# Rows normalised on ScalarE, a gate bias in 16-bit halves, a re-ordered last stage and a summary taken in pairs of tiles, in a two-layer attention and FFN kernel

## What is computed

```python
# layer 0 attention: softmax over 1601 context keys + 256 causal keys, 16 heads of 128, 4 key/value heads
q, k = rope(rms_norm(x @ wq)), rope(rms_norm(x @ wk)); k_ctx = rms_norm(ctx @ wk_ctx)
out = softmax(q @ [k_ctx, k].T * scale + mask) @ [ctx @ wv_ctx, x @ wv] @ wo
# layer 0 FFN: rows rotated by a Hadamard matrix, quantised to 8 bits; weights ternary
h = silu(bitlinear(x, w_gate)) * bitlinear(x, w_up); out = bitlinear(h, w_down)
# layer 1 attention: linear attention over the context, phi(x) = x + 1 if x > 0 else exp(x)
k, v = split(ctx @ Wkv.T); kv_summary = einsum('bhsd,bhse->bhde', phi(k), v); k_sum = phi(k).sum(-2)
gate = sigmoid(x @ Wg.T + bg)
attn = (phi(x @ Wq.T) @ kv_summary) / (phi(x @ Wq.T) . k_sum + eps); out = (attn * gate) @ Wo.T
# layer 1 FFN: 8 experts, top 2 per row by a softmax router
```

## Time and profile before

| | |
|---|---|
| median of 3 runs | 1352.47 us (1347.48 to 1353.33) |
| the profiled execution | 1355.68 us, of which its span is 1353.6 us |
| PE busy | 1215.0 us, 90% |
| DVE busy | 1021.0 us, 75% |
| ACT busy | 823.1 us, 61% |
| POOL busy | 761.6 us, 56% |

### The profile page before, as it was taken

How to read it: one execution, slowest core, us unless ns; L and a number is a source line. 1 busy time by engine, 2 the same in 40 slices (tenths; PEclk the granted TensorE clock), 3 DMA queues, 4 the chain that set the end, 5 groups by cost and what they waited for, 6 DMA issues and landing times.

```text
span 1353.6 us, 30595 instructions
## 1 busy us (share of the span) xinstructions
PE 1215.0 (90%) x11443; PEld 914.0 (68%) x11443; DVE 1021.0 (75%) x2067; ACT 823.1 (61%) x1916; POOL 761.6 (56%) x964
## 2 busy tenths in 40 slices
PE   3888789999999999999999999999999556778898
PEld 2555467877777777877778777777777444455557
DVE  5777678788878887878788788877888485973654
ACT  3555577767767676676767677677676452453331
POOL 2000386857758586675867658586686375822210
PEclk9999899999999999999999999999999787886899
DMA  7531068687977879788786876878778891000000
GB/s 250 169 102 38 1 118 148 125 148 136 178 144 126 141 128 145 133 177 138 136 148 125 140 137 126 147 122 151 137 130 148 177 214 26 1 1 1 0 1 31
DMA packets 499933, 156.99 MB, mean 116 GB/s; under 512 B 484800, under 2 KB 493776, under 8 KB 499792
## 3 DMA queue, kind: packets, MB, share of 16 engines
q1 hardware_dynamic: 497664, 147.77, 58.9%
q0 software_dynamic: 2128, 7.35, 2.1%
HBM read 29.12 MB, written 4.33 MB: 25 GB/s over the span
## 4 chain that ended last, share of the span: by engine, by line
PE 67%; DVE 15%; DMA 6%; POOL 5%; ACT 4%; issue 3%; SPq 0%; POOLq 0%; ACTq 0%; DVEq 0%
PE PS L1164 13%; PE PS L1166 13%; PE PS L1165 13%; PE PS L1320 7%; PE PS L1316 7%; PE PS L1317 7%; DVE mx L1648 4%; DMA pT_h<-ph 3%; DMA pT_l<-pl 2%; DVE pl L1668 2%; POOL xn L891 2%; PE PS L1269 1%; PE PS L665 1%; ACT ctx_h L1393 1%; POOL rstd L888 1%
## 5 line engine op out<-in xcount | busy, mean ns | idle before, releaser
L1648 DVE TENSOR_REDUCE mx<-PS 128x1 f32<-128x512 f32 (+2 forms) x512 | 297.0, 622 | 137.6 <-PE PS L1166 136.4
L1316 PE MATMUL PS<-v_h,pT_h 128*128 128x129 f16 (+1 forms) x1856 | 229.4, 224 | 23.2 <-DMA pT_h<-ph 13.7
L1317 PE MATMUL PS<-v_l,pT_h 128*128 128x128 f16 (+1 forms) x1856 | 229.4, 222 | 0.0
L1864 POOL CAST ph<-pr_end 128x705 f16<-128x705 f32 (+1 forms) x128 | 109.1, 853 | 184.5 <-ACT pr_end L1459 171.7
L1316 PEld LDWEIGHTS PS<-v_h,pT_h 128*128 128x128 f16 (+1 forms) x1856 | 184.5, 99 | 27.5 <-DMA pT_h<-ph 15.2
L1164 PE MATMUL PS<-kT_h,qT_h 128*128 128x512 f16 (+2 forms) x512 | 182.0, 356 | 7.3 <-ACT pr L1459 7.3
L1317 PEld LDWEIGHTS PS<-v_l,pT_h 128*128 128x128 f16 (+1 forms) x1856 | 184.7, 100 | 2.5
L1459 ACT ACTIVATE pr<-PS,nb 128x1024 f32<-128x1024 f32 x128 | 144.0, 1125 | 64.9 <-DVE nb L1656 64.9
L1165 PE MATMUL PS<-kT_l,qT_h 128*128 128x512 f16 (+2 forms) x512 | 181.2, 354 | 0.0
L1166 PE MATMUL PS<-kT_h,qT_l 128*128 128x512 f16 (+2 forms) x512 | 181.1, 354 | 0.0
L1668 DVE TENSOR_TENSOR pl<-pr,ph 128x1024 f16<-128x1024 f32 x128 | 172.5, 1348 | 0.0
(11 more groups left out here) (287 smaller groups left out, 2969.4 us busy)
## 6 DMA issues: line engine op xcount, KB each, us to landing
stage<-in_ctxT SPq DMA_DIRECT2D x8, 800.5 KB, 5.3
lanes<-in_w_lanes SPq DMA_DIRECT2D x16, 192.0 KB, 4.2
stage<-in_wq SPq DMA_DIRECT2D x4, 512.0 KB, 3.7
stage<-in_wo SPq DMA_DIRECT2D x4, 512.0 KB, 3.9
pT_h<-ph SPq DMA_TRANSPOSE x128, 4.3
pT_l<-pl SPq DMA_TRANSPOSE x128, 4.2
ctx_kept<-ctx_h SPq DMA_DIRECT2D x2, 800.5 KB, 6.7
ctx_kept<-ctx_l SPq DMA_DIRECT2D x2, 800.5 KB, 8.3
```

What stands on the lines that cost most here:

```text
L1316: mm(PS[:, OB, 0:DH + 1], pT_h[0:rows, slot, t, :], v_h[0:rows, par, v, :], start=t == 0, stop=False)
L1317: mm(PS[:, OB, 0:DH], pT_h[0:rows, slot, t, :], v_l[0:rows, par, v, :], start=False, stop=False)
L1648: dve.reduce_max(mx[:, c:c + 1], PS[:, c, 0:cols(u % LT, c)], AX_X).then_inc(mx_part, 1)
L1864: pool.tensor_copy(ph[:, slot, HALF:LAST + w], pr_end[:, 0:BANK + w]).then_inc(pool_hi, 1)
```

## The change

- The summary runs in 28 steps of up to two tiles (seven to a sequence, the 65-row tile last). ACT reads k from PSUM twice, for exp(k/64 + ln 64) and for relu(k), and casts v to float16; DVE takes min(exp, 64) + relu in one operation, and v's low half; POOL casts the sum to float16 and subtracts for its low half; PE adds three float16 products instead of one float32 product. All is scaled by 64, and the summary by 1/64 at the end. Some buffers are three deep, and the summary of a step is issued after the projection two steps later.
- The loop starts as soon as items 0, 1 and 2 are split. SP issues Wkv's load ahead of x's. The normalising and transposing of x stand inside the first steps, the products for the rope tables inside POOL's steps 7 to 10, the other splits after steps 0, 2, 3 and 5 of each sequence.
- In the last stage POOL makes per row the factor and a shift, -mean * factor (`row_scales`, two more small operations), and ACT normalises: Identity with scale and bias. `nm` moves from TAIL_POOL to TAIL_ACT.
- The gate's bias is two float16 rows, added by two float16 matmuls.
- TAIL_PE, TAIL_ACT and TAIL_DVE have new orders, the splitting of the last group's ternary weights comes after that unit's `out_norm`, and `dn1:03` (so half 0's last `az`) is the last step of all.
- The first preparing jobs take other PSUM banks.

```diff
-    qt:12 qt:13 dn0:10 dn0:11 lq:00 dn0:12 dn0:13 lq:01 tr1:10 tr1:11 la:00 la:01 la:02 la:03 lg:10
...
+    dn0:11 tr1:01 dn0:12 dn0:13 lq:00 lq:01 tr1:10 lg:00 tr1:11 lg:01 lg:10 lg:11 la:00 la:01 la:02
+    la:03 lq:10 lq:11 tr3:00 tr3:01 lo:00 lo:01 la:10 la:11 la:12 la:13 tr2:00 tr3:10 tr2:01 tr3:11
...
+    nm0:00 nm0:01 hi0:00 hi0:01 cq:00 cq:01 nm0:10 si0:00 hi0:10 nm0:11 si0:01 hi0:11 si0:02 si0:03
+    cq:10 cq:11 hx0:00 si0:10 hx0:01 si0:11 hx0:02 si0:12 hx0:03 si0:13 hx0:10 hx0:11 ro:00 ro:01 hx0:12
+    hx0:13 ro:02 ro:03 ct:00 ct:01 ct:02 ro:10 ro:11 ct:03 nm1:00 hi1:00 ro:12 ro:13 ct:10 ct:11 nm1:01
+    ct:12 ct:13 hi1:01 nm1:10 lc:00 lc:01 hi1:10 nm1:11 sg:00 hi1:11 sg:01 ex:00 ex:01 sg:10 sg:11 lc:10
...
-    nm0:00 nm0:01 nm0:10 nm0:11 b1:00 b1:01 bp:01 b1:02 b1:03 bp:03 b1:10 b1:11 bp:11 b1:12 b1:13 bp:13
...
+    rs0:00 rs0:01 rs0:10 rs0:11 b1:00 b1:01 bp:01 b1:02 b1:03 bp:03 b1:10 b1:11 bp:11 b1:12 b1:13 bp:13
...
+L1_STEPS = (CT + 1) // 2
+L1_ALL = B * L1_STEPS
+L1_LOADS = {0: 0, 2: 1, 3: 2, 5: 3}
+LN_AT = 2
...
-                after(B - 1)
+        def l1_tiles(n):
+
+            t = n % L1_STEPS
+            return [((2 * t + j) * P, P) for j in range(2)] if t < L1_STEPS - 1 else [((CT - 1) * P, CREM)]
+
+        def l1_shape(n):
+            tiles = l1_tiles(n)
+            return len(tiles), tiles[0][1]
+
...
                     o = token_tile(hf, 0, j)
-                    mm(o, ones[0:1, :], bgs[:, :], start=True, stop=False)
+                    mm(o, ones16[:, :], bg_h[:, :], start=True, stop=False)
+                    mm(o, ones16[:, :], bg_l[:, :], start=False, stop=False)
                     for c in range(DC):
...
+            def norm(n, hf, p):
+                act.wait_ge(tl[f"rs{n}"], nth(f"rs{n}", hf, p))
+                for j in (2 * p, 2 * p + 1):
+                    t = hf * 4 + j
+                    last = act.activation(xn4[hf][:, j, :], x_tile(hf, j), ACT.Identity, scale=rstd[:, t:t + 1],
+                                          bias=shift[:, t:t + 1])
+                last.then_inc(tl[f"nm{n}"], 1)
...
-                for j in (2 * p, 2 * p + 1):
-                    t = hf * 4 + j
-                    last = pool.tensor_scalar(xn4[hf][:, j, :], x_tile(hf, j), mv[:, t, 0:1], rstd[:, t:t + 1],
-                                              ALU.subtract, ALU.mult)
-                last.then_inc(tl[f"nm{n}"], 1)
+                step(pool.tensor_tensor(shift[:, at], mv[:, at, 0], rstd[:, at], ALU.mult))
+                pool.tensor_tensor(shift[:, at], shift[:, at], minus[:, at], ALU.mult).then_inc(tl[f"rs{n}"], 1)
...
-                         x.rearrange("(t p) d -> p t d", p=P)).then_inc(in_x, 16)
             for i, (parts, n, scale, hi, lo) in enumerate(loads):
+                if i == 1:
+                    sp.dma_start(xs[:, :].rearrange("p (t d) -> p t d", t=TILES),
+                                 x.rearrange("(t p) d -> p t d", p=P)).then_inc(in_x, 16)
...
+            def l1_proj(n):
+                b = n // L1_STEPS
+                if n % L1_STEPS == 0:
+                    pe.wait_ge(set_lo, FIRST if b == 0 else FIRST + 4 * (b - 1) + 2)
+                wait(pe, l1_vl, n - 1)
+                for j, (col, rows) in enumerate(l1_tiles(n)):
+                    for c in range(DC):
+                        last = three(PS[0:rows, n % 2 * 2 + j, :],
...
-                              vf_s[0:nrows, par, c, :], start=first, stop=final)
+            def l1_summary(n):
+                b, t, slot = n // L1_STEPS, n % L1_STEPS, n % 3
+                m, rows = l1_shape(n)
+                if t == 0:
+                    wait(pe, l1_R, b - 1)
+                    if b == 1:
+                        pe.wait_ge(ln_lo, 4)
+                pe.wait_ge(l1_vl, n + 1)
+                pe.wait_ge(l1_lo, n + 1)
+                for j in range(m):
+                    for c in range(DC):
+                        o = PS[:, (TB, OB)[b % 2] + c, :]
+                        fh, fl = (f[0:rows, slot, j, c * P:(c + 1) * P] for f in (f_h, f_l))
+                        mm(o[:, 0:129], fh, w_vh[0:rows, slot, j, c, :], start=t + j == 0, stop=False)
+                        mm(o[:, 0:128], fh, w_vl[0:rows, slot, j, c, :], start=False, stop=False)
+                        last = mm(o[:, 0:129], fl, w_vh[0:rows, slot, j, c, :], start=False, stop=t == L1_STEPS - 1)
                 last.then_inc(l1_sum, 1)
...
+            pe.wait_ge(in_const, 16)
+            for n in range(L1_ALL + 2):
+                if n < L1_ALL:
+                    l1_proj(n)
+                if LN_AT <= n < LN_AT + 4:
+                    turn_x(n - LN_AT)
+                if n >= 2:
+                    l1_summary(n - 2)
...
+                m, rows = l1_shape(n)
+                b0 = n % 2 * 2
                 act.wait_ge(l1_mm, n + 1)
-                wait(act, l1_k, n - 1)
-                copy(k_s[0:nrows, par, :], PS[0:nrows, SB + par, 0:256], 1 / WS).then_inc(l1_copy, 1)
-                act.wait_ge(l1_min, n + 1)
-                act.activation(ex_s[0:nrows, par, :], ex_s[0:nrows, par, :], ACT.Exp).then_inc(l1_exp, 1)
+                wait(act, l1_phi, n - 1)
+                k = PS[0:rows, b0:b0 + m, 0:256]
+                act.activation(ex_s[0:rows, n % 2, 0:m, :], k, ACT.Exp, bias=lnws[0:rows, :], scale=1 / WS)
+                act.activation(re_s[0:rows, n % 2, 0:m, :], k, ACT.Relu).then_inc(l1_relu, 1)
+                wait(act, l1_sum, n - 2)
+                copy(w_vh[0:rows, n % 3, 0:m, :, 0:P],
+                     PS[0:rows, b0:b0 + m, 256:512].rearrange("p j (c e) -> p j c e", c=DC), 1 / WS).then_inc(l1_vh, 1)
 
             act.wait_ge(made_const, 1)
-            l1_walk(act, l1_step, set_hi_part)
+            for n in range(L1_ALL):
+                l1_step(n)
+                if LN_AT <= n < LN_AT + 4:
+                    x_hi(n - LN_AT)
+                for i in l1_load(n):
+                    set_hi_part(i)
 
 
...
+                    if last and u == UNITS - 2:
+                        norm(0, 0, 0)
+                        norm(0, 0, 1)
...
-
-                dve.tensor_scalar_min(ex_s[0:nrows, par, :], k_s[0:nrows, par, :], 0.0).then_inc(l1_min, 1)
-                wait(dve, l1_sum, n - 1)
-                dve.tensor_scalar(vf_s[0:nrows, par, :, 0:P],
-                                  PS[0:nrows, SB + par, 256:512].rearrange("p (c n) -> p c n", c=DC),
-                                  1 / WS, None, ALU.mult).then_inc(l1_v, 1)
...
-                                         ex_s[0:nrows, par, :], ALU.max, ALU.add).then_inc(l1_k, 1)
+            def l1_step(n):
+                m, rows = l1_shape(n)
+                b0 = n % 2 * 2
+                dve.wait_ge(l1_relu, n + 1)
+                wait(dve, l1_lo, n - 1)
+                dve.scalar_tensor_tensor(f_s[0:rows, n % 2, 0:m, :], ex_s[0:rows, n % 2, 0:m, :], WS,
+                                         re_s[0:rows, n % 2, 0:m, :], ALU.min, ALU.add).then_inc(l1_phi, 1)
+                dve.wait_ge(l1_vh, n + 1)
+                wait(dve, l1_sum, n - 2)
+                dve.scalar_tensor_tensor(w_vl[0:rows, n % 3, 0:m, :, :],
+                                         PS[0:rows, b0:b0 + m, 256:512].rearrange("p j (c e) -> p j c e", c=DC), 1 / WS,
+                                         w_vh[0:rows, n % 3, 0:m, :, 0:P], ALU.mult, ALU.subtract).then_inc(l1_vl, 1)
...
                         job()
+                    if last:
+                        out_norm(g, u)
+                        for kind, i in jobs_of(u, g):
+                            if kind == "weight":
...
-                        dve.tensor_scalar(bgs[:, :], bgs[:, :], WS, None, ALU.mult).then_inc(tw_made, 1)
+                        dve.memset(ones16[:, :], 1.0)
+                        link(dve.tensor_scalar(bg_h[:, :], bgs[:, :], WS, None, ALU.mult))
+                        dve.scalar_tensor_tensor(bg_l[:, :], bgs[:, :], WS, bg_h[:, :], ALU.mult, ALU.subtract)\
+                           .then_inc(tw_made, 1)
...
-                    out_norm(g, u)
+                    if not last:
+                        out_norm(g, u)
...
+                                       nwb[:, k, o:o + 64], ALU.mult).then_inc(tab_made, 1)
+
+            def l1_step(n):
+                m, rows = l1_shape(n)
+                pool.wait_ge(l1_phi, n + 1)
+                wait(pool, l1_sum, n - 2)
+                f, hi, lo = f_s[0:rows, n % 2, 0:m, :], f_h[0:rows, n % 3, 0:m, :], f_l[0:rows, n % 3, 0:m, :]
+                pool.tensor_copy(hi, f).then_inc(l1_hi, 1)
+                pool.wait_ge(l1_hi, n + 1)
+                pool.tensor_tensor(lo, f, hi, ALU.subtract).then_inc(l1_lo, 1)
...
                         rope(e, to) if isinstance(e, str) else pieces(e, to)
+                    if last and u == UNITS - 2:
+                        row_scales(0, 0, 0)
...
```

255 lines of the change are left out of this document (113 added, 142 removed).

## The result

| | before | after |
|---|---|---|
| median | 1352.9 us (4 runs, 1347.5 to 1353.9) | 1308.6 us (4 runs, 1305.1 to 1313.4) |
| the profiled execution, its span | 1355.7 us, 1353.6 us | 1307.2 us, 1305.4 us |
| PE, DVE, ACT, POOL busy | 1215, 1021, 823, 762 us | 1194, 1017, 839, 797 us |

The ratio is 0.968 (95% interval 0.964 to 0.972): 44 us faster, where 42 were forecast, 1310 us. One run of experiment 1 (1596 us) and one run of the kernel before beside it (3734 us) were disturbed and are counted nowhere. The forecast is right in its sum. Its terms are not: the last stage's gain was put down to the wrong parts of the change.

What follows compares the result with a forecast made beforehand. PE comes close to bounding the first loop; in the last stage PE's low clock and POOL's normalising cost time. 1355.7 - 22.5 - 21.5 + 1.5 = 1313.2 profiled, 1310 as median; range about 1298 to 1326, widened to 1294 and 1332.

Steps and rivals of the forecast that it cites:

- The loop's start: First stage: the summary's loop begins at 16.3 us instead of 24.41, as casts follow x's load at once; 8.0 us saved.
- PE's work in the loop: First stage: pairs of tiles at 3.28 us and four single tiles take 85.3 us against 90.5; 5 us saved.
- The waits: First stage: contention of DVE and POOL takes 4 us (0 to 8), the drain leaves PE idle some 1.6.
- rival A: First stage: exclusion of DVE and POOL sets the pace, 97 us of operations; gain 13 instead of 22.5, 1319 us; chance 0.16.
- Normalising: Last stage: ACT instead of POOL normalises six pairs of row tiles on the path; 7 us saved.
- Bias and clock: Last stage: float16 bias matmuls end two stretches at clock 0.50, of 12 and 18 us; 13.8 us saved, bias included.
- cold starts of 8 us: Last stage, a lower case for bias and clock: cold starts of 8 us instead of 4, saving 9.9.
- The orders: Last stage: new step orders bring `ga1:00` some 23 us earlier, taken as the same gain seen otherwise; nothing added.
- the 0.7 before 1196: Before 1196 us, where DVE is busiest: 0.7 us saved from the earlier nm0.
- Rival B: Last stage: new orders leave short waits and the clock stays low; 7 + 5.7 saved, 1319 to 1322 us; chance 0.15.
- The output stores: End of the kernel: both stores start after the very last step; 1.5 us lost, bounds 0 to 4.5.
- The last group: Two ternary weights, 2 x 2.1 us, behind the last out_norm, offset by an earlier nm0; between -1.5 and +3, taken as 0.

Runs made afterwards that it cites:

- experiment 1: The kernel after with the gate's bias in float32 again, all else kept: 1315.2 us, ratio to before 0.969.
- experiment 5: The kernel after with the old last-stage orders of PE, ACT and DVE and the float32 bias again: 1332.6 us, last part 225.0.
- experiment 10: The kernel after with one SBUF input for DVE's f, rope-table operations spread over POOL's steps 7 to 18, the loop's last split one step earlier: 1303.2 us.

## Why the prediction was right, and where it was not

**The loop's start.** Forecast 16.3, measured 15.7. Right, step by step: cast and low half follow the load at once.

**PE's work in the loop.** A pair of tiles takes 3.27 us in the undisturbed timeline (107.06 to 110.33), forecast 3.28. Right.

**The waits.** The prediction allowed 4 us for contention and 1.6 for the drain. PE waited 8.4 us for f_l and 2.1 for w_vl. This term was too small by 4.9; the start and the work were better than forecast by 1.8, and the preparing matmuls came at 118.7 instead of 115.6. So this stage brought 19.4 us for 22.5. The mechanism was named: DVE with two SBUF inputs and POOL hold each other up. What I had not placed is where it hurts: at POOL's steps with the rope tables, which I had as "some 7 us" in rival A only, and at the end of the loop, where no buffer is left to hide behind. Rival A is refuted in its main point, for the pace is set by PE at 3.27 us a pair, and not by 97 us of exclusive operations; yet a third of its loss is there.

**The Trainium skill's rule of exclusion** (SBUF — State Buffer, section Who interferes with whom) was left open for a loop. It holds there: f with two SBUF inputs 905 ns, with one 644, while the subtraction on POOL, 1.16 us alone, takes 2.0 to 2.8 beside a split.

**Normalising, booked at 7.** Worth 4.8 in the new orders and 5.3 in the old ones. The mechanism is right, its price was not: I took 0.37 us for 256 columns from a copy out of PSUM with fixed operands. ACT's instruction takes 0.594 (24 of them, 583 to 601 ns), 1.09 a pair; with that the prediction's own sum gives 14.5 - 6.5 - 2.5 - 0.9 = 4.6. The Trainium skill, ScalarE: Activation LUTs, section What ACT_TABLE_LOAD costs, has the sum: 186 ns and 0.833 ns a column, and 93 ns for each operand that is one value per partition; the estimate from it for 256 columns and two such operands is 585 ns. The trace agrees with it, and the prediction did not use it.

**Bias and clock, booked at 13.8.** Worth 10.0 in the old orders, which is the prediction's own 9.9 for cold starts of 8 us, and 2.1 to 3.4 in the new ones. The step that failed is "the stretches at 0.50 with PE busy that are longer than 8 us are just those with the float32 row of one partition in them". That was a coincidence read as a cause. With all float32 rows in the new orders the clock stays at 1.00; without any, in the old orders, there is still a stretch of 10 us. The kernel before has one too: from 1265.5 to 1275.0 the clock is at 0.50 with PE busy for 7.0 us and no such row, and the earlier trace rows shows only its end. What holds is less: where the clock is down, the rows keep it down for longer.

**The orders, booked at nothing.** Worth 12.2. My walk through the four tables gave `ga1:00` some 23 us earlier with 3 us of its work done already. Measured from the last 1/sum it comes 12.0 us earlier, 16.6 without the new wait for ternary weights, and the part behind it is 6.3 shorter. The walk had found the gain. I then wrote that it was "the same gain seen from the other side", and gave it to bias and normalising. That is true of some 6 us, which either the bias or the orders bring (the orders 18.5 with the float32 bias and 12.2 without it), and false of the 12 that come on top. Bias and orders together brought 22.0, from 225.0 (experiment 5) to 203.0, the later stores included, where 13.8 - 1.5 = 12.3 was booked. Two terms were booked too high: normalising, with the 0.7 before 1196, by 2.4, and the ternary weights, at nothing, by the 9.1 that their new place costs in the old orders. The errors, 9.7 more than booked, 2.4 and 9.1 less, nearly cancel in the sum.

**Rival B, the clock stays low.** Refuted for the new orders. It is what happens in the old ones: counted in steps of 2 us, the last part spends 46 us at 0.50 in the kernel before, 38 with ScalarE and halves in the old orders, and 20 in the kernel after (32 in experiment 10, with the same last stage).

**The output stores, booked at 1.5 more.** From the last issue to the end of the span it is 4.9 us for 3.4. Right.

**The last group, booked at nothing, from -1.5 to 3.** It gained 9.9 us. The two ternary weights behind the last `out_norm` make PE wait 4.6, as 2 x 2.1 had it, but that the clock is lower behind that wait (9.1 us in all in the old orders, 3.4 in the new ones) and what they no longer hold up (7.5 to 9.4 us of waits for o_s) was not in the sum. With the weights put back the balance is about zero, as forecast. The kernel of the first stage alone gains 6.5 us in this group, and its waits for transposes fall from 13.8 to 5.9 us. The kernel after waits 17.9 us for them, more than the kernel before, and gains by the waits for o_s (9.4 to nothing) and for normalised rows (7.4 to 0.3). The prediction had no view on the transposes: it said of the softmax stage that it was not touched.

**In sum.** Forecast 22.5, 20.0 and nothing for first stage, last stage and last group; measured 19.4, 18.3 and 9.9, and 0.6 in between. The sum came out since the last group gave more than what the others fell short of. The profiled execution took 1307.2 us for a sum of 1313.2; 1310 was within 2 us of the median because the median of the kernel before lies 3.2 below its profiled execution and that of the kernel after 1.4 above. With terms wrong by 8 to 12 us that is luck; the range, made of the bounds of each, is what deserved trust.

## What to carry to other kernels

When two parts of a change act on the same waits, price each by a kernel in which it stands alone before you credit it; a walk through the order of the steps and a sum over instructions are two counts of different things, and what one finds beyond the other is a term of its own. To take a new wait out of a comparison, don't subtract its length, for here a wait of 4.6 us cost 9.1: compare from a step behind it on. An instruction inside a stretch at a low clock is its cause only if a kernel with that instruction and without the waits ahead of it is slow too. Where two engines exclude each other, the time is lost anyway; put the meeting at steps with spare buffers behind them, and keep it from the loop's end.

## What was not expected of the hardware

A float32 matmul with one row of one partition leaves the granted clock at 1.00 when PE has had no wait ahead of it (18 us with eight pairs of 0.69 us), but where the clock is at 0.50 already it stays there past them (15 us for 6 with the 16-bit halves). A short wait of PE can cost twice its length: one of 4.55 us cost 9.1 up to the first gate row in the old orders, with PE's mean clock at 0.84 instead of 0.92. Small operations on POOL pay for exclusion out of proportion: the four of 128 columns for the rope tables took 0.46 to 2.04 us in the kernel after, 1.36 on average, and 0.45 in experiment 10, where they met no operation of DVE with two inputs in SBUF. A DMA transpose of the probabilities landed after 17.1 and 18.4 us in two profiles of the kernel before, beside weight loads issued by POOL, against a median of 4.3; in the twelve other kernels the same transpose landed after 7.3 to 12.6 us, against a median of 3.6.
